# First mixture of a two-layer attention and mixture-of-experts kernel: order of the one-hot comparisons on VectorE and of the row transposes on TensorE

## The reference, cut to what matters

```python
scores = jax.nn.softmax(xf @ gate_w.T, axis=-1)
_, idx = jax.lax.top_k(scores + gate_b, K)              # K = 6 of E = 64
xb = jnp.zeros((E, CAP, D), xf.dtype).at[se, pos].set(xf[tok], mode='drop')   # CAP = 64 rows an expert
h = jax.nn.silu(jnp.einsum('ecd,eid->eci', xb, w1)) * jnp.einsum('ecd,eid->eci', xb, w3)
yb = jnp.einsum('eci,edi->ecd', h, w2)
y = jnp.zeros_like(xf).at[tok].add(contrib * wf[:, None])
```

## Time and profile before

| | us |
|---|---|
| median of three runs (332.26 to 333.8) | 333.51 |
| the profiled execution | 332.18 |
| its span, first to last instruction | 330.4 |
| TensorE matmul busy | 273.7 (83%) |
| VectorE busy | 227.4 (69%) |
| ScalarE busy | 166.6 (50%) |
| GpSimd busy | 160.6 (49%) |
| mean granted TensorE clock | 0.924 |

### The profile page before, as it was taken

How to read it: one execution, slowest core, us unless ns; L and a number is a source line. 1 busy time by engine, 2 the same in 40 slices (tenths; PEclk the granted TensorE clock), 3 DMA queues, 4 the chain that set the end, 5 groups by cost and what they waited for, 6 DMA issues and landing times.

```text
span 330.4 us, 6098 instructions
## 1 busy us (share of the span) xinstructions
PE 273.7 (83%) x2180; PEld 187.6 (57%) x2180; DVE 227.4 (69%) x575; ACT 166.6 (50%) x323; POOL 160.6 (49%) x184
## 2 busy tenths in 40 slices
PE   1996766788989899987359999999898989899970
PEld 0665435367778778865112545554466667679740
DVE  2467889445675564437488777875648788999793
ACT  1455230342354235533232777778686978678830
POOL 5856373854234419426305433302271079977772
PEclk9999955999999999999755899999999999999995
DMA  6972294348996554230421500002300002500044
GB/s 205 305 258 100 63 189 76 41 40 212 207 195 163 147 149 34 86 107 1 111 66 37 128 18 4 1 3 87 110 15 4 0 21 57 165 0 12 27 139 128
DMA packets 22569, 30.66 MB, mean 93 GB/s; under 512 B 2926, under 2 KB 15135, under 8 KB 22283
## 3 DMA queue, kind: packets, MB, share of 16 engines
q1 hardware_dynamic: 19835, 26.46, 27.9%
q0 software_dynamic: 1920, 2.90, 8.0%
q10 hardware_dynamic: 784, 0.92, 0.9%
HBM read 23.19 MB, written 7.92 MB: 94 GB/s over the span
## 4 chain that ended last, share of the span: by engine, by line
PE 51%; DVE 17%; POOL 9%; issue 9%; DMA 7%; ACT 5%; DVEq 0%; SPq 0%; POOLq 0%; ACTq 0%
PE bank L922 43%; PE bank L1119 3%; POOL ew L616 2%; DVE score L1863 2%; POOL dispatched L671 2%; DMA packc<-in_packc 2%; DMA big<-q_parts 1%; DMA ew<-normalised,slot_token 1%; PE bank L1131 1%; ACT ctxT L796 1%; DMA returned_last<-ctxT,big 1%; POOL rstd L563 1%; POOL returned L683 1%; POOL big L626 1%; DMA ks<-returned_last 1%
## 5 line engine op out<-in xcount | busy, mean ns | idle before, releaser
L922 PE MATMUL bank<-frbuf,splits 128*128 128x512 f32 (+1 forms) x240 | 60.9, 388 | 2.0 <-DVE frbuf L1915 1.7
L616 POOL DMA_INDIRECT ew<-normalised,slot_token x32 | 33.1, 1036 | 43.7 <-DVE slot_token L1633 36.0
L1863 DVE TENSOR_REDUCE score<-bank 128x2 f32<-128x512 f32 x64 | 42.2, 687 | 14.4 <-PE bank L922 13.7
L922 PEld LDWEIGHTS bank<-frbuf,splits 128*128 128x128 f32 x240 | 41.9, 188 | 13.6 <-DVE frbuf L1915 3.9
L879 ACT ACTIVATE pbuf<-bank 128x512 f32<-128x512 f32 x64 | 37.1, 598 | 16.0 <-PE bank L922 15.6
L1915 DVE TENSOR_TENSOR frbuf<-pbuf,frbuf 128x512 fp32r<-128x512 f32 (+1 forms) x48 | 36.6, 775 | 5.6 <-ACT pbuf L907 5.1
L1639 DVE CAST splits<-bank 128x1024 fp32r<-128x1024 bf16 x16 | 19.6, 1223 | 25.8 <-PE bank L922 21.5
L903 ACT ACTIVATE frbuf<-bank,biases 128x512 fp32r<-128x512 f32 (+1 forms) x48 | 30.6, 638 | 11.0 <-PE bank L922 10.1
L922 PE MATMUL bank<-ks,big 128*128 128x256 bf16 x128 | 29.5, 323 | 6.4 <-DVE score L1863 3.7
L922 PE MATMUL bank<-splits,frbuf 128*128 128x512 f32 (+1 forms) x144 | 32.0, 373 | 0.8 <-ACT frbuf L824 0.8
L907 ACT ACTIVATE pbuf<-bank,biases 128x512 f32<-128x512 f32 (+1 forms) x48 | 30.3, 631 | 0.0
(11 more groups left out here) (222 smaller groups left out, 538.7 us busy)
## 6 DMA issues: line engine op xcount, KB each, us to landing
big<-in_w SPq DMA_DIRECT2D x8, 704.0 KB
ew<-in_ew SPq DMA_DIRECT2D x16, 256.0 KB, 3.5
big<-in_w SPq DMA_DIRECT2D x8, 352.0 KB
ks<-k_parts SPq DMA_DIRECT2D x4, 512.0 KB, 8.1
k_parts<-parts SPq DMA_DIRECT2D x2, 768.0 KB, 3.8
big<-q_parts SPq DMA_DIRECT2D x8, 192.0 KB
returned<-vbuf SPq DMA_DIRECT2D x1, 1024.0 KB, 15.2
ks<-returned SPq DMA_DIRECT2D x4, 256.0 KB, 3.7
```

The lines of the kernel that those rows point to most:

```text
L616: pool.indirect_dma_start(out=xg[:, g % 2, j, :], out_offset=None, in_=xn_dram, in_offset=bass.IndirectOffsetOnAxis(ap=slot_token[:, g % 3 ...
L922: return pe.matmul(out_, lhsT, rhs, start=start, stop=stop, skip_group_check=True)
L1863: v.tensor_reduce(nm1[:, c, 2 * hp:2 * hp + 2], bank[m % 2][:, :].rearrange("p (h k) -> p h k", h=2), X, ALU.max, negate=True).then_inc(a_ ...
```

## The change: what it does

On TensorE `combine(g - 1)` goes behind `gathered_transposes(g + 1)`. On VectorE, for groups 1 to 4, both halves of the one-hot matrix of group g + 3 are made by one instruction, ahead of the first copy `dispatch_even(g, 0)`. In group 0 the second half goes ahead of `yl`.

```diff
                 if g == 0:
                     shared_outputs(1)
-                else:
-                    combine(g - 1)
                 if g + 1 < NG:
                     gathered_transposes(g + 1)
                 if g >= 1:
+                    combine(g - 1)
                     dispatch_transposes(g, 1)
...
                 if g >= 1:
                     if g + 2 < NG:
                         slot_values(g + 2)
+                    if g + 3 < NG:
+                        dispatch(g + 3)
                     dispatch_even(g, 0)
-                if g + 3 < NG:
+                else:
                     dispatch(g + 3, range(0, 4))
                 dispatch_even(g, 2)
+                if g == 0:
+                    dispatch(g + 3, range(4, 8))
 
                 v.wait_ge(e_yh, g + 1)
                 v.tensor_tensor(out=yl, in0=bank[7][:, :].rearrange("p (j d) -> p j d", j=NPAIR),
                                 in1=yh.bitcast(F32), op=ALU.subtract).then_inc(e_yl, 1)
-                if g + 3 < NG:
-                    dispatch(g + 3, range(4, 8))
```

## The result

| us | before | after |
|---|---|---|
| median of five executions | 333.51 | 347.81 |
| lowest and highest | 332.26 to 334.89 | 340.27 to 348.59 |
| the profiled execution | 332.18 | 345.16 |
| its span | 330.4 | 343.2 |
| mean granted TensorE clock | 0.924 | 0.904 |

The changed kernel takes 1.0267 times as long, 95% interval 1.0207 to 1.0327. Three of its five executions lie more than 1.5% above the fastest and are left out of that ratio, so it rests on two (345.16 and 340.27), and the medians stand further apart than it says. Slower was forecast, but at 336.5 and at most 339.5: the sign is right, the size far too small.

What follows compares the result with a forecast made beforehand. TensorE's chain of waits through every group was taken to bound the kernel. Terms -4.8 + 1.1 + 2.4 + 3.0 + 0 + 1.7 + 0.1 = +3.5 us, on the mean of 332.9, gave 336.5; range 332.5 to 339.5.

Steps and rivals of the forecast that it cites:

- (a): TensorE's wait for the comparison ahead of the slot numbers, 0.96 us, falls away five times: -4.8 us.
- (b): TensorE's new order: a wait for VectorE's copy replaces that for ScalarE's, +0.19 in six groups: +1.1 us.
- The hold: On GpSimd, the early comparison makes the first gather issue of four take 3.0 us instead of 0.94.
- The rival in which GpSimd isn't held: GpSimd's gather issues are not delayed by the early comparison: sum +0.2, 333.1 us; chance 0.14.
- (c): Turn of group 1: TensorE waits for group 2's rows, whose last gather lands 5.5 us after issue: +2.4 us.
- (d): Turn of group 2: TensorE, ready at 88.8, waits for group 3's delayed rows, landing at 91.8: +3.0 us.
- (e): Rows of group 4, wanted by TensorE at 102.0, land just in time: 0, at most +2.8 us.
- (f): Rows of group 5 land 11.3 to 12.5 us after the slot numbers, against a group of 10.2: +1.7 us.
- The clock: Rival: TensorE's granted clock falls after waits in group 2, costing some 3 us: 339.4 us; chance 0.10.

Runs made afterwards that it cites:

- In pieces: The changed kernel with the early comparison in eight instructions of 128x512 instead of one of 128x4096: 341.79 us, ratio 0.9956 to the kernel before.

## Why the prediction was wrong in size

(a) and (b) held: no comparison wait, 0.49 for VectorE's copy in each turn, 10.16 a turn for 10.22. The hold was priced rightly as well: 2.75 for the 3.0 given, the end 0.82 behind the comparison. The rival in which GpSimd isn't held fell. That the sign came out right is not luck: in the trace as in the forecast the waits for rows outweigh what is saved, and those of turns 1 and 5 stand where they were forecast. (The mean of 332.9 plus 3.5 is 336.4, not 336.5; nothing hangs on it.)

(c) is the step that failed: "This part of the program is as before", and so the landing 5.5 after the issue. It isn't as before: the change moves group 0's second comparison ahead of `yl`, next to this very issue. The landing time was taken over from the trace before as if it were the gather's own. It was that of a gather which ran just ahead of a weights load. In the changed kernel the issue is held for 0.84 and the weights come 0.58 earlier, and the load is in front: 9.5 instead of 5.5, a wait of 7.1 instead of 2.4. Of these 4.7 us, 4.1 are the later landing and 0.6 is that TensorE comes earlier. Weights behind the rows give 2.05, near what was forecast, and this is shown; a queue without the zeros didn't help. What puts the load in front differs: on the first chip the unheld issue is late too, on the third the hold alone does it. In both traces of the kernel before the gather was in front, which is why they gave no warning; with TensorE's order of before and the weights in front, the run of VectorE's order alone waited 3.4. The point between 0.2 and 0.9 us at which one order turns into the other was not looked for.

(d) named a real cost at the wrong time. It does not occur in the change (-3.0), since TensorE comes 5.6 us later than (d) has it (slot numbers done at 94.41 for 88.8), while the rows landed at 90.6 for the 91.8 given; it does occur (3.6) where turn 1 is as short as (c) had it. (e), priced at 0 with +2.8 as its bound, came at 2.4, near its bound, and (f), 1.7, at 2.8. After (d) had fallen out, the turns alternated: a turn of 10.2 is too short for the hold and a landing of 5.8 or 6.2 with weights issued 0.15 behind the end of the gather's issue, a lengthened one leaves the next enough. In pieces both waits are 0.3 or less, which shows the hold in them.

The clock was the rival with 0.10, priced at 3 for one fall. It came three times, 5.7 in all. Against it I had argued that the groups around are full of work; the wait in group 1 alone was enough. In the run with only TensorE's order 0.80 and 1.17 us close together were, while one of 1.91 in the run with late weights was not, so the length of a short wait doesn't tell. Without the clock the loss would have been 8.2, so the miss of 10.4 in the account is one half (c) to (f) and one half the clock. They are not two causes: the clock falls because of the waits, and leaves with them.

## What to carry to other kernels

A landing time read from a trace belongs to the order in which transfers reach the queues, not to the transfer. Before work is taken away from in front of a small gather, ask which large load will be issued near it, and tie that load behind the gather: here one wait on SyncE took 5 to 7.5 us off the stretch, depending on the trace of the change it is set against. A wait that a dense TensorE stretch did not have before should be priced with its own length and, as a case of its own, with the slower clock behind it: 1.4 to 2.9 us here where it came, whether the wait was 1.2 or 7 us long.

## What the runs showed of the hardware

- The last gather of four, its issue ended 0.2 us behind the issue of a weights load on SyncE's queue, went first and landed in 5.5 and 5.3 (before, and TensorE's order alone); ended 0.9 us and more behind, it landed in 8.2 to 9.7 (four kernels), while its rows came only when the load had moved data for some 4 us. The Trainium skill, "DMA: Bandwidth & Descriptors", section "Queues, rings and completion order", says that a DMA engine takes turns between the queues that have work, packet by packet. By that rule a gather of 0.07 MB would slip in between early; the windows above show no rows of it for those microseconds, and no run here tells whether its descriptors were late or stood back.
- A GpSimd indirect DMA issue that meets a VectorE comparison already running with both inputs in SBUF lasts until 0.82 us after it. Eight instructions of 512 columns, one after another with the same total, hold it for only 0.27 and the next issue for 0.1.
- The granted clock fell to 0.50 in each wait of TensorE for rows of 2.0 us and more (2.04 to 6.94, brackets of the timeline). Of the shorter ones it fell at 1.17 (with one of 0.80 just before), 1.28, 1.45 and 1.81, and not at 0.92, 1.02, 1.25, 1.63 and twice 1.91, nor at 1.47 to 1.53 ahead of the slot numbers. Where the combine followed, it and the four transposes together took 1.4 to 2.9 us longer, so some 3 to 6 us ran at half speed.
- The same kernel's median differed by 2.6% between chips. On the third the groups of the kernel before are 4.5 us longer, with ScalarE's copies starting 0.6 late in its turns; the free turns of the changed kernel are not longer there.
